# Attention over 96 token chunks: the maximum is subtracted inside the stream of the next logit and value products

## The chip, the core and the metric

The kernel runs on one core of a Trainium2 chip. The metric is the device time of one execution in microseconds (us), as the median of several runs. The engines of the core run side by side, each through its own list of instructions in order, and wait for one another by semaphores: TensorE (PE in the profile, its weight loads PEld), VectorE (DVE), ScalarE (ACT), GpSimd (POOL) and SyncE (SP).

## The reference, cut to what matters

The whole model is a chain of a convolution, a delta-rule attention, an expert-choice layer, an attention over video embeddings and a mixture of experts. The change lies in the attention over the video:

```
t = layer_norm(text_embeds, ln1_g, ln1_b)
vd = layer_norm(video_embeds, ln1_g, ln1_b)
q = (t @ Wq.T + bq).reshape(T, Nw, HEADS, HEAD_DIM)
k = (vd @ Wk.T + bk).reshape(V, Fr, HEADS, HEAD_DIM)
v = (vd @ Wv.T + bv).reshape(V, Fr, HEADS, HEAD_DIM)
logits = jnp.einsum('avhd,bthd->abhvt', k, q) / math.sqrt(HEAD_DIM)
weights = jax.nn.softmax(logits, axis=3)
attn = jnp.einsum('avhd,abhvt->abhtd', v, weights)
attn = attn.transpose(0, 1, 3, 2, 4).reshape(V, T, Nw, EMBED)
attn = attn.mean(axis=0)
o = attn @ Wo.T + bo
```

There are 64 videos (a) of 12 frames (v) and 2 heads (h) of 64. Each token takes a softmax over the 12 frames of every video and head, and the weighted values are averaged over the videos.

## The kernel before

`attention_phase` works on 96 chunks of 128 tokens (16 batches of 6 chunks). For one chunk the logits lie in three PSUM banks: the partitions are 2 heads times 64 videos, the free axis is 12 frames times 128 tokens. Two sets of three banks alternate from chunk to chunk; bank 6 gathers the products with the values, and bank 7 serves three purposes in turn: the transpose of normed tokens ("turn", line 367), the query projection (line 1667) and the output projection (lines 1726 and 1727).

The work on one chunk is spread over several steps, and each engine has a loop over the step n, written out by hand; there is no scheduler.

- TensorE, step n: for each of the 12 frames, the logits of chunk n (line 1689) and the products of chunk n-4 with the values (line 1697), as 64x64 pieces of the array side by side. Then, in the steps that have one, a turn or a query projection for a later batch. Then the subtraction of the maximum of chunk n-1 (line 1715): three products with an identity in bf16 add the negated maximum to the logits in PSUM ("shift" from here on). Then the output projection of chunk n-5, which writes bank 7.
- VectorE, step n: two small sums for the denominator of chunk n-2 (lines 1584, 1588), the negated maximum over the frames of chunk n (line 1592, it reads PSUM), and the product of the exponentials of chunk n-2 with the reciprocal denominator (line 1596, two inputs from SBUF).
- ScalarE, step n: the copy of chunk n-6's output (line 1628), the copy of chunk n-4's value sums out of bank 6 ("aT", line 1632), in some steps the copy of a turn (line 381, "a_xT") or of a query (line 1613, "qT") out of bank 7, then the three exponentials of chunk n-1 (line 1641), one for each bank, each released by one shift, then the reciprocal of chunk n-2's denominator (lines 1648, 1650), and in some steps the norm of tokens (line 1607).
- GpSimd: one addition for each chunk, of one half of its exponentials to the other (line 1661).

Turns stand in the steps n with n mod 12 = 1, 3, 7 or 9 and queries in those with n mod 12 = 2, 4, 8 or 10, as long as there is a next batch: 30 of each. Of any six steps in a row in the steady state two hold a turn, two a query and two neither ("plain" steps). Turn, query and output projection share bank 7, so in a step with a turn or a query the output projection waits until ScalarE has copied the bank out:

```
if now:
    pe.wait_ge(nt.moved, now[0] * 4 + now[1] + 1)
elif before:
    pe.wait_ge(q_ready, before[0] * 4 + before[1] + 1)
elif o:
    pe.wait_ge(o_ready, o)
```

Here `now` is a turn in this step, `before` a query, `nt.moved` counts the copies of line 381, `q_ready` those of line 1613. The output projection begins with n = 5.

Of the kernel before, what the change touches and what calls it, by code (L numbers as in the profile page):

```python
# [8 lines left out]
ACT = mybir.ActivationFunctionType  # L9
# [4 lines left out]
P = 128  # L14
# [8 lines left out]
NCH = B * NC  # L23
# [1501 lines left out]
def attention_phase(nc, k):  # L1525
# [6 lines left out]
    with stack:  # L1532
        nt = NormTranspose(nc, k, "a_", sb, sem)
        qT = sb("qT", [P, 2, TP])
        nm = sb("nm", [P, 2, P], BF16)
        eb = sb("eb", [P, 4, FR, P])
# [7 lines left out]
        q_ps, q_ready, q_bias, l_ps, m_ready, shifted, e_ready = (  # L1544
            sem(x) for x in ("q_ps", "q_ready", "q_bias", "l_ps", "nm_ready", "shifted", "e_ready"))
# [4 lines left out]
        FB = FR // 3  # L1550
# [5 lines left out]
        def lbanks(n):  # L1556
            o = 3 * (n % 2) * 512
            return k.psf[:, o:o + FR * P].rearrange("p (v t) -> p v t", t=P)
# [4 lines left out]
        def place(n, hd):  # L1563

            return half(hd if n // 4 % 2 == 0 else 1 - hd)
# [9 lines left out]
        with nc.Block() as block:  # L1575
# [25 lines left out]
            @block.scalar  # L1601
            def _(act):
                def norm(i, g):
                    for j in range(GC):
                        c = (g % 2) * GC + j
                        at = i * ST + (g // 2) * NC + c
                        last = nc.scalar.activation(nt.xl[:, g, j, :], k.h[:, i * 2 + g // 2, c, :], ACT.Identity,
                                                    scale=k.rstd[:, at:at + 1], bias=k.mean[:, at:at + 1])
                    last.then_inc(nt.normed, 1)

                def query(i, g, bank):
                    act.wait_ge(q_ps, i * 4 + g + 1)
                    nc.scalar.activation(qT[:, g // 2, (g % 2) * GW:(g % 2 + 1) * GW], k.ps[:, bank, 0:GW],
                                         ACT.Identity, scale=0.125, bias=bq8[:, 0:1]).then_inc(q_ready, 1)

                nc.scalar.preload_act_table_set("natural_log_exp_and_others")
                for g in range(2):
                    norm(0, g)
                for g in range(2):
                    nt.move(act, 0, g, 6 + g, k.g1[:, 0:1], k.b1n[:, 0:1])  # L1620
                act.wait_ge(q_bias, 2)
                for g in range(2):
                    query(0, g, 4 + g)
                for n in range(NCH + 6):
                    o = n - 6
                    if o >= 0:
                        act.wait_ge(o_ps, o + 1)
                        nc.scalar.activation(big[:, o, :], k.ps[:, 7, 0:P], ACT.Copy).then_inc(o_ready, 1)
                    a = n - 4
                    if 0 <= a < NCH:  # L1630
                        act.wait_ge(a_ps, a + 1)
                        nc.scalar.activation(aT[:, a % 2, :], k.ps[:, 6, 0:P], ACT.Copy).then_inc(a_ready, 1)
                    if slot(n):
                        nt.move(act, *slot(n), 7, k.g1[:, 0:1], k.b1n[:, 0:1])
                    if slot(n - 1):
                        query(*slot(n - 1), 7)
                    e = n - 1
                    if 0 <= e < NCH:
                        for s in range(3):
                            act.wait_ge(shifted, 3 * e + s + 1)  # L1640
                            nc.scalar.activation(eb[:, e % 4, s * FB:(s + 1) * FB], lbanks(e)[:, s * FB:(s + 1) * FB],  # L1641
                                                 ACT.Exp).then_inc(e_ready, 1)
                    w = n - 2
                    if 0 <= w < NCH:
                        act.wait_ge(summed, w + 1)
                        if w >= 2:
                            act.wait_ge(w_ready, w - 1)
                        nc.scalar.activation(rd[:, w % 2, :], den[:, w % 2, :], ACT.Ln).then_inc(logged, 1)
                        act.wait_ge(logged, w + 1)
                        nc.scalar.activation(rd[:, w % 2, :], rd[:, w % 2, :], ACT.Exp, scale=-1.0).then_inc(rd_ready, 1)  # L1650
                    if slot(n + 1):
                        norm(*slot(n + 1))
# [10 lines left out]
            @block.tensor  # L1663
            def _(pe):
                def query(i, g, bank):
                    pe.wait_ge(nt.moved, i * 4 + g + 1)
                    nc.tensor.matmul(k.ps[:, bank, 0:GW], k.wq[:, :], nt.xT[:, g // 2, (g % 2) * GW:(g % 2 + 1) * GW],
                                     start=True, stop=True).then_inc(q_ps, 1)

                for g in range(2):  # L1670
                    nt.turn(pe, 0, g, 6 + g)
                for g in range(2):
                    query(0, g, 4 + g)
                pe.wait_ge(q_bias, 2)
                for n in range(NCH + 5):
                    a = n - 4
                    logits, values = n < NCH, 0 <= a < NCH
                    if logits and n % NC == 0:
                        pe.wait_ge(q_ready, n // NC * 2 + 2)
                    if values:  # L1680
                        pe.wait_ge(w_ready, a + 1)
                        if a:
                            pe.wait_ge(a_ready, a)
                    for v in range(FR):
                        if logits:
                            if v % FB == 0 and n >= 2:
                                pe.wait_ge(e_ready, 3 * (n - 2) + v // FB + 1)
                            for hd in range(2):
                                last = nc.tensor.matmul(  # L1689
                                    lbanks(n)[place(n, hd), v, :], k.Kt[half(hd), v, :],  # L1690
                                    qT[half(hd), n // NC % 2, (n % NC) * P:(n % NC + 1) * P],
                                    start=(v % FB == 0), stop=True, skip_group_check=True)
                            if v == FR - 1:
                                last.then_inc(l_ps, 1)
                        if values:
                            for hd in range(2):
                                last = nc.tensor.matmul(  # L1697
                                    k.ps[half(hd), 6, 0:P], k.Vd[place(a, hd), v, half(hd)],
                                    eb[place(a, hd), a % 4, v, :], start=(v == 0), stop=(v == FR - 1))
                            if v == FR - 1:  # L1700
                                last.then_inc(a_ps, 1)
                    now, before, o = slot(n), slot(n - 1), n - 5
                    if now or before:
                        if o >= 1:
                            pe.wait_ge(o_ready, o)
                        if before:
                            query(*before, 7)
                        if now:
                            if o < 1 and n > 1:
                                pe.wait_ge(q_ready, now[0] * 4 + now[1])  # L1710
                            nt.turn(pe, *now, 7)
                    if 1 <= n <= NCH:
                        pe.wait_ge(m_ready, n)
                        for s in range(3):
                            nc.tensor.matmul(lbanks(n - 1)[:, s * FB:(s + 1) * FB, :], k.identb[:, :],
                                             nm[:, (n - 1) % 2, None, :].to_broadcast([P, FB, P]), start=False, stop=True,
                                             skip_group_check=True).then_inc(shifted, 1)
                    if 0 <= o < NCH:
                        pe.wait_ge(a_ready, o + 1)
                        if now:  # L1720
                            pe.wait_ge(nt.moved, now[0] * 4 + now[1] + 1)
                        elif before:
                            pe.wait_ge(q_ready, before[0] * 4 + before[1] + 1)
                        elif o:
                            pe.wait_ge(o_ready, o)
                        nc.tensor.matmul(k.ps[:, 7, 0:P], one[0:1, :], k.bo1[0:1, :], start=True, stop=False)
                        nc.tensor.matmul(k.ps[:, 7, 0:P], aT[:, o % 2, :], k.wo1[:, :],
                                         start=False, stop=True).then_inc(o_ps, 1)
# [655 lines left out]
```

## Time and profile before

| | |
|---|---|
| median of 3 runs | 2298.33 us (2295.48 to 2301.55) |
| the profiled execution | 2295.3 us |
| its span, first to last instruction | 2293.4 us |
| TensorE busy in the span | 2042.9 us (89%) |
| VectorE busy | 1628.5 us (71%) |
| ScalarE busy | 1075.9 us (47%) |
| GpSimd busy | 608.5 us (27%) |
| attention loop | from 1062 to 1543 us of the span |

These shares are averages over stages with different limits; the attention is some 480 us of the 2293. In the views of the timeline each row has the start, the length, the engine, the source line, the operation with its output and input, and the number of instructions merged; in brackets stands idle time of the engine ahead of it and what ended it. A group of x2 matmuls of line 1689 runs beside an equal group of line 1697, and 24 such pairs of groups make the logits and values of one step.

### The profile page before, as it was taken

Reading aid. Unit: us, or ns where it says so; the run is one execution under the profiler, and the core shown is the slowest. Engines: PE = TensorE matmul, PEld = TensorE weight load, DVE = VectorE, ACT = ScalarE, POOL = GpSimd, SP = SyncE. Lnnn points to the kernel's source line nnn. Section 1 sums busy time; section 2 is a strip of 40 time slices with the busy share of each in tenths; the row PEclk is TensorE's granted clock in tenths of the full one; section 3 lists DMA queues with packets and bytes.
Section 4 is the critical chain, followed back from the end, with each engine's and each line's share of the span. In section 5 each row is a group of like instructions: output and inputs, shape, how many; then the busy total and the mean of one; then the engine's idle time right before and its main releaser. Section 6 shows DMA issues by size and latency. Waiting matters only on the chain. (4 is left out here: it accounts for less than half of the span.)

```text
span 2293.4 us, 54841 instructions
## 1 busy us (share of the span) xinstructions
PE 2042.9 (89%) x20986; PEld 1801.0 (79%) x20986; DVE 1628.5 (71%) x4183; ACT 1075.9 (47%) x2698; POOL 608.5 (27%) x650
## 2 busy tenths in 40 slices
PE   6699999989747888986999999985999999999998
PEld 5488777778536878874777777775999999999998
DVE  4755556554583855665999999987777777777773
ACT  4433333332344555644666666642444444444443
POOL 0002222220025555511333333333212221221220
PEclk9799999999868999998999999997999999999999
DMA  8100000100211111100000000000000000000000
GB/s 184 42 1 12 11 11 11 15 8 1 76 56 40 42 34 40 41 10 2 3 3 3 3 3 3 3 2 1 8 8 14 7 7 14 7 7 14 7 8 14
DMA packets 80356, 44.52 MB, mean 19 GB/s; under 512 B 45800, under 2 KB 74024, under 8 KB 79752
## 3 DMA queue, kind: packets, MB, share of 16 engines
q1 hardware_dynamic: 74248, 29.53, 5.7%
q0 software_dynamic: 5888, 12.07, 2.0%
q8 instruction: 137, 2.24, 0.4%
q14 instruction: 83, 0.68, 0.1%
HBM read 27.20 MB, written 14.38 MB: 18 GB/s over the span
## 5 line engine op out<-in xcount | busy, mean ns | idle before, releaser
L2105 ACT ACTIVATE w<-banks,b 128x384 f32<-128x384 f32 (+1 forms) x512 | 259.7, 573 | 393.0 <-PE banks L2179 393.0
L2161 PE MATMUL banks<-w,w 128*128 128x128 f32 (+1 forms) x3072 | 364.1, 275 | 0.0
L2161 PEld LDWEIGHTS banks<-w,w 128*128 128x128 f32 (+1 forms) x3072 | 350.4, 189 | 9.1 <-issue 8.7
L1689 PE MATMUL banks<-qT,w 64*64 64x128 f32 x4608 | 272.2, 271 | 3.2 <-ACT eb L1641 2.4
L1697 PE MATMUL banks<-eb,w 64*64 64x128 f32 x4608 | 272.4, 271 | 0.2 <-DVE eb L1596 0.2
L1689 PEld LDWEIGHTS banks<-qT,w 64*64 64x64 f32 x4608 | 249.3, 133 | 16.6 <-DVE eb L1596 2.2
L1661 POOL TENSOR_TENSOR t<-eb 128x768 f32<-128x768 f32 x96 | 174.6, 1819 | 309.2 <-ACT eb L1641 299.3
L1697 PEld LDWEIGHTS banks<-eb,w 64*64 64x64 f32 x4608 | 249.2, 133 | 0.9 <-DVE eb L1596 0.8
L2002 DVE SCALAR_TENSOR_TENSOR h<-banks,t_wt,h 128x128 f32 (+3 forms) x672 | 183.8, 344 | 83.1 <-PE banks L2161 79.7
L1237 POOL DMA_INDIRECT xg<-xs,rowu x184 | 179.5, 976 | 127.0 <-DMA xg<-xs,rowu 84.7
L1596 DVE TENSOR_TENSOR eb<-eb,rd 128x1536 f32<-128x1536 f32 x96 | 208.6, 2172 | 2.1 <-ACT rd L1650 2.1
L2177 PE MATMUL banks<-t_xh,t_w1h 128*128 128x384 f32 (+1 forms) x512 | 182.5, 356 | 0.1
L1592 DVE TENSOR_REDUCE nm<-banks 128x128 bf16<-128x1536 f32 x96 | 167.8, 1748 | 10.8 <-PE banks L1689 10.8
L2179 PE MATMUL banks<-t_xh,t_w1l 128*128 128x384 f32 (+1 forms) x512 | 171.7, 335 | 0.0
L2178 PE MATMUL banks<-t_xlo,t_w1h 128*128 128x384 f32 (+1 forms) x512 | 171.0, 334 | 0.0
L2045 POOL TENSOR_TENSOR t_rstd<-t_nv,t_minus_half 128x6 f32<-128x6 f32 x48 | 63.6, 1326 | 399.7 <-DVE t_nv L1903 398.3
L1641 ACT ACTIVATE eb<-banks 128x512 f32<-128x512 f32 x288 | 150.5, 598 | 0.0
L1183 DVE SCALAR_TENSOR_TENSOR x_yl<-banks,gates,x_yh 128x128 fp32r<-128x128 f32 x184 | 52.0, 345 | 129.3 <-ACT x_yh L1330 129.1
L1428 PE MATMUL banks<-x_sel,x_yh 128*128 128x374 f32 (+1 forms) x384 | 119.7, 393 | 2.1 <-ACT x_oT L1339 1.9
L1191 DVE TENSOR_SCALAR x_sel<-iota,place 128x748 fp32r<-128x748 f32 x184 | 104.6, 622 | 6.3 <-PE banks L1428 6.2
L729 ACT ACTIVATE DT<-banks 128x768 f32<-128x768 f32 x60 | 48.7, 811 | 123.6 <-PE banks L822 123.6
L1428 PE MATMUL banks<-x_sel,x_yl 128*128 128x374 f32 (+1 forms) x384 | 98.8, 339 | 0.0
(300 smaller groups left out, 4325.3 us busy)
## 6 DMA issues: line engine op xcount, KB each, us to landing
out<-h SPq DMA_DIRECT2D x16, 320.0 KB
xs<-r_xl SPq DMA_DIRECT2D x16, 192.0 KB, 2.8
h<-in_xT SPq DMA_DIRECT2D x4, 750.0 KB, 14.8
h<-in_xT SPq DMA_DIRECT2D x4, 749.0 KB, 17.6
xg<-xs,rowu POOLq DMA_INDIRECT x184
xs<-r_xl SPq DMA_DIRECT2D x16, 128.0 KB
blocks<-NT SPq DMA_DIRECT2D x24, 48.0 KB, 1.9
D<-blocks SPq DMA_DIRECT2D x24, 48.0 KB, 2.1
```

Of the source, the lines that this page charges most:

```text
L1237: nc.gpsimd.indirect_dma_start(out=xg[:, 4 * g + j, :], out_offset=None, in_=k.xs, in_offset=bass.IndirectOffsetOnAxis(ap=rowu[:, col:col ...
L1428: last = nc.tensor.matmul(k.ps[:, 5 + s, 0:TW // 2], y[lo:hi, col % 8, :], sel[lo:hi, col % SEL, s * (TW // 2):(s + 1) * (TW // 2)], start ...
L1596: nc.vector.tensor_tensor(eb[:, w % 4], eb[:, w % 4], rd[:, w % 2, None, :].to_broadcast([P, FR, P]), ALU.mult).then_inc(w_ready, 1)
L1661: nc.gpsimd.tensor_tensor(t1[:, n % 2], e[:, 0:6], e[:, 6:12], ALU.add).then_inc(tree, 1)
L1689: last = nc.tensor.matmul(lbanks(n)[place(n, hd), v, :], k.Kt[half(hd), v, :], qT[half(hd), n // NC % 2, (n % NC) * P:(n % NC + 1) * P], s ...
L1697: last = nc.tensor.matmul(k.ps[half(hd), 6, 0:P], k.Vd[place(a, hd), v, half(hd)], eb[place(a, hd), a % 4, v, :], start=(v == 0), stop=(v ...
L2002: last = nc.vector.scalar_tensor_tensor(out=hh, in0=k.psf[0:n, o:o + P], scalar=wt[0:n, par, c * E1 + e:c * E1 + e + 1], in1=hh if e else ...
L2105: nc.scalar.activation(gb[u % 2][:, f, s * GW:s * GW + NFREE[s]], k.ps[:, order.bank(n), 0:NFREE[s]], ACT.Relu, bias=k.b1_1[:, 2 * e + f:2 ...
L2161: last = nc.tensor.matmul(k.psf[0:n, o:o + P], gb[u % 2][:, f, c * P:c * P + n], k.w2_1[:, 2 * e + f, :], start=(f == 0), stop=(f == 1))
L2177: nc.tensor.matmul(ps, w1h[:, 2 * e + f, :], xh[:, g, 0:w], start=True, stop=False)
L2178: nc.tensor.matmul(ps, w1h[:, 2 * e + f, :], xlo[:, g, 0:w], start=False, stop=False)
L2179: nc.tensor.matmul(ps, w1l[:, 2 * e + f, :], xh[:, g, 0:w], start=False, stop=True).then_inc(full, 1)
```

## The change

On TensorE the shift of chunk n-1 moves from behind the turn or query of step n into the loop over the frames: ahead of frame 8 of 12, the last third of the logits and values. It still waits for the same maximum. On ScalarE the three exponentials of chunk n-1 move ahead of the copies aT, a_xT and qT of the same step; only the output copy of line 1628 still stands ahead of them. For the first output projection (chunk 0), which followed a query of the step before, a wait for that query's copy is written out. Nothing is added to or taken from the arithmetic.

```diff
@@ scalar @@
                     a = n - 4
+                    e = n - 1
+                    if 0 <= e < NCH:
+                        for s in range(3):
+                            act.wait_ge(shifted, 3 * e + s + 1)
+                            nc.scalar.activation(eb[:, e % 4, s * FB:(s + 1) * FB], lbanks(e)[:, s * FB:(s + 1) * FB],
+                                                 ACT.Exp).then_inc(e_ready, 1)
                     if 0 <= a < NCH:
                         act.wait_ge(a_ps, a + 1)
                         nc.scalar.activation(aT[:, a % 2, :], k.ps[:, 6, 0:P], ACT.Copy).then_inc(a_ready, 1)
...
                     if slot(n - 1):
                         query(*slot(n - 1), 7)
-                    e = n - 1
-                    if 0 <= e < NCH:
-                        for s in range(3):
-                            act.wait_ge(shifted, 3 * e + s + 1)
-                            nc.scalar.activation(eb[:, e % 4, s * FB:(s + 1) * FB], lbanks(e)[:, s * FB:(s + 1) * FB],
-                                                 ACT.Exp).then_inc(e_ready, 1)
@@ tensor @@
+                def shift(e):
+                    pe.wait_ge(m_ready, e + 1)
+                    for s in range(3):
+                        nc.tensor.matmul(lbanks(e)[:, s * FB:(s + 1) * FB, :], k.identb[:, :],
+                                         nm[:, e % 2, None, :].to_broadcast([P, FB, P]), start=False, stop=True,
+                                         skip_group_check=True).then_inc(shifted, 1)
...
                     for v in range(FR):
+                        if v == 2 * FB and 1 <= n <= NCH:
+                            shift(n - 1)
                         if logits:
...
-                    if 1 <= n <= NCH:
-                        pe.wait_ge(m_ready, n)
-                        for s in range(3):
-                            nc.tensor.matmul(lbanks(n - 1)[:, s * FB:(s + 1) * FB, :], k.identb[:, :],
-                                             nm[:, (n - 1) % 2, None, :].to_broadcast([P, FB, P]), start=False, stop=True,
-                                             skip_group_check=True).then_inc(shifted, 1)
                     if 0 <= o < NCH:
...
                         elif o:
                             pe.wait_ge(o_ready, o)
+                        else:
+                            pe.wait_ge(q_ready, 4)
```

TensorE in step 7, the first steady step with a turn, in the kernel before. The names are the output and input tiles (`a_xl` the normed tokens, `nm` the negated maxima, `eb` the exponentials), `nm_ready` tells of a maximum, `a_moved` of a copy of a turn, `ao_ready` of an output copy:

```order
L1697 MATMUL banks<-eb,w_0 64x128 x2
L367 MATMUL banks<-ident,a_xl 128x128 [waits a_normed,ao_ready]
L367 MATMUL banks<-ident,a_xl 128x128 x2
L1715 MATMUL banks<-nm,identb 128x512 [waits nm_ready]
L1715 MATMUL banks<-nm,identb 128x512 x2
L1726 MATMUL banks<-bo,one 128x128 [waits a_moved,a_ready]
L1727 MATMUL banks<-wo,aT 128x128
```

The same step of TensorE in the changed kernel, from the shift on; the rows left out are the rest of the last third of logits and values:

```order
L1673 MATMUL banks<-nm,identb 128x512 [waits nm_ready]
L1673 MATMUL banks<-nm,identb 128x512 x2
L1698 MATMUL banks<-qT,w_0 64x128 [waits e_ready]
L1698 MATMUL banks<-qT,w_0 64x128
L1706 MATMUL banks<-eb,w_0 64x128 x2
...
L367 MATMUL banks<-ident,a_xl 128x128 [waits a_normed,ao_ready]
L367 MATMUL banks<-ident,a_xl 128x128 x2
L1731 MATMUL banks<-bo,one 128x128 [waits a_moved,a_ready]
L1732 MATMUL banks<-wo,aT 128x128
```

The shift no longer stands between the turn and the output projection that waits for the turn's copy; it now splits the run of 64-row products.

ScalarE in the same step before, where `shifted` tells of a shift, `a_ps` of finished value sums and `a_turned` of a turn:

```order
L1628 ACTIVATE o_all<-banks 128x128 [waits ao_ps]
L1632 ACTIVATE aT<-banks 128x128 [waits a_ps]
L381 ACTIVATE a_xT<-banks,b1n,g 128x384 [waits a_turned]
L1641 ACTIVATE eb<-banks 128x512 [waits shifted] x3
L1648 ACTIVATE rd<-den 128x128 [waits aw_ready,summed]
```

And in the changed kernel:

```order
L1628 ACTIVATE o_all<-banks 128x128 [waits ao_ps]
L1634 ACTIVATE eb<-banks 128x512 [waits shifted] x3
L1638 ACTIVATE aT<-banks 128x128 [waits a_ps]
L381 ACTIVATE a_xT<-banks,b1n,g 128x384 [waits a_turned]
L1648 ACTIVATE rd<-den 128x128 [waits aw_ready,summed]
```

The exponentials went past two copies, each of which TensorE waits for: aT in the next step, a_xT in this one.

## Rows read from the trace of the kernel before

**Rows 1.** Windows: length; busy us (count) of PE, PEld, DVE, ACT, POOL; granted clock; DMA.

```profile
850.00:900.00 50.00, 42.68 (x258) 38.84 (x258) 28.06 (x75) 26.72 (x80) 28.46 (x31) 0.97 0.15 40
...
1100.00:1500.00 400.00, 390.89 (x8558) 299.06 (x8554) 397.19 (x328) 268.44 (x707) 148.38 (x83) 1.00 0.01 3
```

**Rows 2.** Waits, 1100 to 1520: total us, times, longest.

```profile
PE banks L1726 <- ACT a_xT L381: 5.6, 27, 0.2
...
PEld banks L1715 <- DVE nm L1592: 0.5, 3, 0.2
```

**Rows 3.** Timeline of TensorE around a plain step.

```profile
1150.20 0.28 PE L1689 MATMUL banks<-qT,w 64*64 64x128 f32 x2
...
1150.42 0.82 PE L1715 MATMUL banks<-nm,identb 128*128 128x512 bf16 x3
1151.17 0.48 PE L1726 MATMUL banks<-bo,one 1*128 1x128 f32 x2
...
1152.01 0.33 PE L1689 MATMUL banks<-qT,w 64*64 64x128 f32 x2
...
1152.17 0.28 PE L1689 MATMUL banks<-qT,w 64*64 64x128 f32 x2
```

**Rows 4.** Timeline of TensorE and ScalarE in the next step, which has a turn.

```profile
1154.57 0.28 PE L1689 MATMUL banks<-qT,w 64*64 64x128 f32 x2
...
1154.88 0.55 PE L367 MATMUL banks<-ident,a_xl 128*128 128x128 f32 x3
...
1155.26 0.81 PE L1715 MATMUL banks<-nm,identb 128*128 128x512 bf16 x3
1155.46 0.67 ACT L381 ACTIVATE a_xT<-banks,b1n,g 128x384 f32<-128x384 f32 x1 [0.23 <-PE banks L367]
1156.04 1.56 ACT L1641 ACTIVATE eb<-banks 128x512 f32<-128x512 f32 x3
...
1156.28 0.45 PE L1726 MATMUL banks<-bo,one 1*128 1x128 f32 x2 [0.21 <-ACT a_xT L381]
```

**Rows 5.** Timeline of TensorE, then ScalarE, in the step after, which has a query.

```profile
1159.64 0.28 PE L1689 MATMUL banks<-qT,w 64*64 64x128 f32 x2
...
1159.86 0.91 PE L1667 MATMUL banks<-a_xT,wq 128*128 128x384 f32 x2
1160.61 0.81 PE L1715 MATMUL banks<-nm,identb 128*128 128x512 bf16 x3
1161.54 0.46 PE L1726 MATMUL banks<-bo,one 1*128 1x128 f32 x2
```
```profile
1160.81 0.58 ACT L1613 ACTIVATE qT<-banks,bq 128x384 f32<-128x384 f32 x1 [0.51 <-PE banks L1667]
```

**Rows 6.** Timeline of TensorE: the shifts of the last plain step and six steps after [rows 3].

```profile
1175.37 0.82 PE L1715 MATMUL banks<-nm,identb 128*128 128x512 bf16 x3
...
1179.73 0.82 PE L1715 MATMUL banks<-nm,identb 128*128 128x512 bf16 x3
```

**Rows 7.** One line's instructions: count, duration min/median/max in ns, first and last start.

```profile
L1596 DVE TENSOR_TENSOR eb<-eb,rd x96: 1742/2279/2930, 1076.2 to 1535.7; 128x1536 f32<-128x1536 f32 x96
```

**Rows 8.** Timeline of VectorE: maxima a step apart, then a stretched product; then GpSimd beside it.

```profile
1148.31 1.75 DVE L1592 TENSOR_REDUCE nm<-banks 128x128 bf16<-128x1536 f32 x1
...
1152.74 1.75 DVE L1592 TENSOR_REDUCE nm<-banks 128x128 bf16<-128x1536 f32 x1
...
1163.79 2.59 DVE L1596 TENSOR_TENSOR eb<-eb,rd 128x1536 f32<-128x1536 f32 x1
```
```profile
1162.93 1.82 POOL L1661 TENSOR_TENSOR t<-eb 128x768 f32<-128x768 f32 x1 [3.44 <-ACT eb L1641]
```

**Rows 9.** Costliest groups of the page: busy, mean ns, idle before and its enders.

```profile
L1689 PE MATMUL banks<-qT,w 64*64 64x128 f32 x4608 | 272.2, 271 | 3.2 <-ACT eb L1641 2.4
```

**Rows 10.** Timeline near the end of the loop: TensorE, then VectorE's last maximum.

```profile
1524.02 0.82 PE L1715 MATMUL banks<-nm,identb 128*128 128x512 bf16 x3
```
```profile
1526.62 1.75 DVE L1592 TENSOR_REDUCE nm<-banks 128x128 bf16<-128x1536 f32 x1
```

## The prediction

> **What bounds the kernel now.** I read the windows of the attention loop first, then the waits, then the timeline step by step. Over 400 us of the loop both TensorE (390.9 us) and VectorE (397.2 us) are busy almost without a gap, at full granted clock (1.00, the upper of the two levels, 2.4 GHz) [rows 1]. So the shares of busy time don't tell which of the two sets the pace. The waits do, together with the lengths. TensorE waits for VectorE's maximum 0.5 us in 420, and 5.6 us for ScalarE's copy of a turn [rows 2]; VectorE waits for nothing at all. Two engines can both run without a wait only if one of them is elastic, and the durations show which. TensorE's instructions keep their lengths from step to step. VectorE's product of line 1596 takes anything from 1.74 to 2.93 us [rows 7]: the one at 1163.79 took 2.59, and beside its first 0.96 us ran GpSimd's addition, which began at 1162.93 and took 1.82 [rows 8]. Without such an overlap VectorE needs 4.43 us a step (1148.31 to 1152.74) [rows 8]. GpSimd's start hangs on TensorE's shift by way of the exponentials. So when TensorE is late against VectorE, the addition slides under the product and slows VectorE down until the two have the same rate. TensorE's list of work sets the rate; VectorE adapts.
>
> TensorE's period is six steps, 29.31 us (shift at 1150.42 to shift at 1179.73) [rows 3, 6]: two steps with a turn, two with a query, two plain. A plain step takes 4.36 us (1175.37 to 1179.73) [rows 6], less than VectorE's undisturbed 4.43, so there the two are nearly even; the average of 4.885 comes from turns and queries.
>
> **What the change costs TensorE.** First the pieces. A pair of groups of logits and values takes 0.109 us (22 of them from 1152.17 to 1154.57) [rows 3, 4], so 24 pairs are 2.62 us and the last third 0.87. Going from them to the shift takes 0.22 instead of 0.11 (1150.20 to 1150.42), so the entry costs 0.11. The three shifts and the way on to the output projection take 0.75 (1150.42 to 1151.17). The first pair after 128-row work takes 0.16 (1152.01 to 1152.17), so the way back costs 0.05 [rows 3]. No row shows a shift followed by a pair; I take 0.75 plus 0.05.
>
> In a *plain* step the shift moves, nothing is hidden by it, and one change of form is added: the values now go straight to the output projection, at 0.11 more as in the steps with a query (1159.64 to 1159.86) [rows 5], and the shift has a way back of 0.05. That is +0.16.
>
> In a step with a *turn* the shift is cover today. The turn begins at 1154.88, the shift at 1155.26, the copy a_xT at 1155.46, and the output projection, which needs the copy, at 1156.28: 1.40 us after the turn began [rows 4]. Without the shift TensorE would be ready 0.38 after the turn began, and the copy can't begin sooner, since it began 0.03 after the turn ended. So the 1.40 stay, about 1.0 of them idle, and the shift's time is added in full where it now stands: 0.11 + 0.75 + 0.05 = +0.91. In a step with a *query* it is the same: query at 1159.86, copy qT at 1160.81, output projection at 1161.54, 1.68 us in all [rows 5], in which the shift of 0.75 was hidden and now isn't: +0.91.
>
> Steps: 30 turns and 30 queries, of which the first two of each lie ahead of the first output projection (step 5) and wait for no copy. That leaves 56 steps at 0.91 = 51.0 us, and of the 91 steps from 5 to 95 there are 35 plain ones at 0.16 = 5.6 us. Six steps would take 29.31 + 4 x 0.91 + 2 x 0.16 = 33.3 us.
>
> **What it gains, and what is hidden.** The exponentials come sooner, by a third of a step or more. TensorE waits for them only at the start of the loop, 2.4 us in all [rows 9]; that goes, less 4 x 0.16: -1.8. At the end VectorE's last maximum begins 2.6 us after the shift that follows the last logits (1526.62 against 1524.02) [rows 10], because VectorE is behind. With TensorE slower VectorE has caught up by then and begins about 0.3 after the logits: -2.3, less up to 0.84 (2.59 against 1.75) [rows 8] if the last addition meets a product: -1.5.
>
> On ScalarE the exponentials now stand ahead of aT, a_xT and qT. Let the shift begin at X. The first of the three ends at X + 0.38 (0.81 for all, at a spacing of 0.22), and the exponentials take 1.56 [rows 4], to about X + 2.0. TensorE ends the last third at X + 0.75 + 0.05 + 0.87 = X + 1.67, begins the turn at about X + 1.9, and a_xT is due 0.58 after that, X + 2.45. In between there is room for aT, so neither copy is late. I cost this part at nothing; the cover is some 0.2 us, and if it failed each late 0.1 us would cost 5.6 us over the 56 steps. The shift's wait for the maximum also comes sooner: after a plain step it stands 0.84 + 0.05 + 1.75 + 0.11 = 2.75 us behind the logits, and the maximum takes 1.75 [rows 8]. 1.0 us is left as long as VectorE isn't behind, and at 4.43 us of work against an average step of 5.5 it isn't. The wait that is written out for the first output projection is for a copy made a step before: nothing. No DMA is issued in the loop.
>
> Sum: 51.0 + 5.6 - 1.8 - 1.5 = +53.3. The profiled execution took 2295.3 us and would take 2348.6; the median of the three runs lies 3.0 above it, at 2298.3, and becomes 2351.6.
>
> The entry of the shift takes 0.11 and the way back from 128-row work 0.05 [rows 3]. The Trainium skill, "TensorEngine Tiling (Array Packing)", section "Key Properties", says that a change of the tiling mode drains TensorE, and it makes no difference between the two directions. The trace agrees that a change costs something and shows the way back as the cheaper one. If the return from the shift cost as much as the entry, 0.06 more in 91 steps would make the sum +59.
>
> *Bounds.* From below: the three shifts at their bare spacing, 0.65, and no cost of changing form, 36 us in the 56 steps and nothing in the plain ones, less 4 at the ends: 2330. From above: a return at 0.15 and aT late by 0.1 make 1.11 in the 56 steps and 0.26 in 35, +71 and -2 at the ends, 2367; and if the idle in each step brought the granted clock to the 0.97 of the stretch where TensorE is busy 85% [rows 1], 3% of some 26 us of streaming in 15 periods adds 11: about 2375.
>
> **Rivals.** *VectorE is the bound (faster).* It is busy 99% of the loop, TensorE's weight loads 299 of 400 us [rows 1]. Then what counts is that GpSimd's addition starts sooner and meets the maximum, which reads PSUM, instead of the product: every step falls to 4.43, 0.455 less in the 84 steps from 5 to 88, -38, or 2260 us. It decides if TensorE has half a microsecond a step to spare. Against it: the maximum that was ready at 1154.49 was used only at 1155.26 [rows 8, 4], and TensorE waited for a maximum 0.5 us in 420 [rows 2]. The Trainium skill, "Perfetto Trace Analysis", section "Identifying the Most-Contended Engine", would have it this way: it judges VectorE by its occupancy and TensorE by its weight loads, not by its matmuls' busy time. I give it 0.08.
>
> *The copies come sooner (no change).* If ScalarE, rid of the exponentials ahead of the output projection, copied bank 7 earlier by the shift's 0.75, nothing would be lost, and the time stays at about 2299. Against it: a_xT follows the turn at once today and qT the query [rows 4, 5]. 0.05.
>
> *The clock falls (slower still).* With about 1 us of idle in four steps of six TensorE's clock might be granted at its lower level for a part. A tenth of the streaming is 2.6 us a period, 38 in all: about 2390. The stretch at 85% has 0.97, though [rows 1]. 0.05.
>
> **How the numbers follow.** The forecast has 0.82, and its bounds, 2330 to 2375, are the range, which leaves the rivals outside. A measurement of this kernel can tell about 0.3% (7 us) from no change. Slower 0.87 (forecast and clock), the same 0.05, faster 0.08.
>
> **What would show it.** In the profile of the changed kernel: six steps in 33.3 us, plain ones 4.5; the waits of the output projection for a_xT and for qT at about 1 us each, 28 times each; the turn still 1.40 ahead of it and the query 1.68; the product of line 1596 mostly near 1.75; idle time of VectorE ahead of the maximum, ended by the logits. The forecast is wrong if the six steps take less than 29.3 us, if the output projection follows the turn sooner than 1.4 us, or if TensorE stands waiting for the maximum ahead of the shift.

## The result, and the profile after

The changed kernel takes 2351.8 us (median of 4 runs, 2346.5 to 2357.3) against 2297.5 us for the kernel before: a ratio of 1.0231, 95% interval 1.0213 to 1.0249. That is 54 us slower; 2352 was forecast.

The profiled execution has a span of 2352.6 us against 2293.4. Of the 59.2 us more, 5.5 lie ahead of the attention loop, where the program is the same: the loop's first turn begins at 1063.4 in place of 1057.9. From that turn to the end of the last output copy the loop takes 538.6 us in place of 485.0, which is +53.6, and what follows the loop takes 750.5 in both. So the change costs 53.6 us, all of it in the loop.

The window that answers to the last of [rows 1], with the same columns:

```profile
1100.00:1500.00 400.00, 361.20 (x7573) 260.45 (x7571) 331.38 (x292) 242.23 (x628) 130.22 (x72) 1.00 0.01 3
```

VectorE was busy 397 us of these 400 before and is now 331; TensorE fell from 391 to 361. The clock is still granted in full. Now VectorE is the one that waits, and the waits between 1100 and 1570 say for whom (total us, times, longest; line 1698 holds the logits, 1731 the output projection):

```profile
DVE nm L1592 <- PE banks L1698: 70.4, 56, 1.3
...
PE banks L1731 <- ACT a_xT L381: 23.9, 28, 0.9
...
PE banks L1731 <- ACT qT L1613: 21.4, 28, 0.8
```

Where TensorE waited 5.6 us for the copies of turns [rows 2], it waits 23.9, and 21.4 for the copies of queries, 28 times each. The timeline of TensorE through a step with a turn and on to the next with a query, to be read beside [rows 4, 5]; line 1673 is the shift:

```profile
1194.61 0.82 PE L1673 MATMUL banks<-nm,identb 128*128 128x512 bf16 x3
...
1198.91 0.28 PE L1698 MATMUL banks<-qT,w 64*64 64x128 f32 x2
...
1199.13 0.82 PE L1673 MATMUL banks<-nm,identb 128*128 128x512 bf16 x3
1199.88 0.33 PE L1698 MATMUL banks<-qT,w 64*64 64x128 f32 x2
...
1200.70 0.28 PE L1698 MATMUL banks<-qT,w 64*64 64x128 f32 x2
...
1200.92 0.55 PE L367 MATMUL banks<-ident,a_xl 128*128 128x128 f32 x3
...
1202.32 0.45 PE L1731 MATMUL banks<-bo,one 1*128 1x128 f32 x2 [0.85 <-ACT a_xT L381]
...
1205.03 0.82 PE L1673 MATMUL banks<-nm,identb 128*128 128x512 bf16 x3
...
1206.82 0.91 PE L1667 MATMUL banks<-a_xT,wq 128*128 128x384 f32 x2
1208.49 0.45 PE L1731 MATMUL banks<-bo,one 1*128 1x128 f32 x2 [0.76 <-ACT qT L1613]
```

The output projection still comes 1.40 us after the turn begins (1200.92 to 1202.32) and 1.67 after the query (1206.82 to 1208.49), as before. But the shift no longer fills that time, and takes 0.75 of its own (1199.13 to 1199.88). A plain step lasts 4.52 (1194.61 to 1199.13). The same step on ScalarE:

```profile
1199.56 1.57 ACT L1634 ACTIVATE eb<-banks 128x512 f32<-128x512 f32 x3 [0.87 <-PE banks L1673]
1201.08 0.28 ACT L1638 ACTIVATE aT<-banks 128x128 f32<-128x128 f32 x1
1201.51 0.67 ACT L381 ACTIVATE a_xT<-banks,b1n,g 128x384 f32<-128x384 f32 x1
```

The exponentials are over at 1201.13, aT follows at once, and a_xT begins at 1201.51, 0.59 after the turn: ScalarE's new order delays nothing. Six steps, from the shift at 1165.93 to that at 1199.13, take 33.20 us in place of 29.31:

```profile
1165.93 0.82 PE L1673 MATMUL banks<-nm,identb 128*128 128x512 bf16 x3
```

### The profile page after: what moved, and what is told of

Same layout as the page of the kernel before. It is cut to its first block and busy times, and to the rows that moved or that the text cites. A ratio compares the mean times of both kernels' runs of the same rounds, so it can differ in the third digit from the quotient of the medians.

```text
span 2352.6 us, 54842 instructions
## 1 busy us (share of the span) xinstructions
PE 2061.3 (88%) x20986; PEld 1794.6 (76%) x20986; DVE 1607.0 (68%) x4183; ACT 1079.9 (46%) x2698; POOL 607.0 (26%) x650
## 5 line engine op out<-in xcount | busy, mean ns | idle before, releaser
L1698 PE MATMUL banks<-qT,w 64*64 64x128 f32 x4608 | 292.8, 273 | 0.8 <-ACT qT L1613 0.8
L1706 PE MATMUL banks<-eb,w 64*64 64x128 f32 x4608 | 292.6, 273 | 0.0
L1596 DVE TENSOR_TENSOR eb<-eb,rd 128x1536 f32<-128x1536 f32 x96 | 176.8, 1841 | 8.4 <-ACT rd L1650 8.4
```

The source lines that it names most:

```text
L1596: nc.vector.tensor_tensor(eb[:, w % 4], eb[:, w % 4], rd[:, w % 2, None, :].to_broadcast([P, FR, P]), ALU.mult).then_inc(w_ready, 1)
L1698: last = nc.tensor.matmul(lbanks(n)[place(n, hd), v, :], k.Kt[half(hd), v, :], qT[half(hd), n // NC % 2, (n % NC) * P:(n % NC + 1) * P], s ...
L1706: last = nc.tensor.matmul(k.ps[half(hd), 6, 0:P], k.Vd[place(a, hd), v, half(hd)], eb[place(a, hd), a % 4, v, :], start=(v == 0), stop=(v ...
```

## Experiments

Two theories run through the first runs. By the forecast's, TensorE's list of work sets the pace and VectorE's product stretches until it fits. By the rival's, VectorE is the bound, as its busy share suggests. Periods of six steps are read from the starts of the shifts in each trace, between steps 24 and 84, and "the loop" is measured as above (485.0 in the trace of the kernel before).

**Half of VectorE's product.**

```diff
-                        nc.vector.tensor_tensor(eb[:, w % 4], eb[:, w % 4],
-                                                rd[:, w % 2, None, :].to_broadcast([P, FR, P]),
+                        nc.vector.tensor_tensor(eb[:, w % 4, 0:6], eb[:, w % 4, 0:6],
+                                                rd[:, w % 2, None, :].to_broadcast([P, 6, P]),
```

> The kernel before, with VectorE's product of line 1596 on 6 of the 12 frames only; the other 6 frames' exponentials stay without their reciprocal denominator, so part of the computation is left out. VectorE has about 0.8 us less to do in each of 96 steps. Theory (TensorE's list sets the pace, VectorE adapts): six steps stay at 29.3 us, the time within 3 us of the kernel before, and VectorE shows idle time instead of stretched products. Rival (VectorE is the bound): its step falls from 4.885 to about 4.1 or less until TensorE's plain 4.4 holds it, so 35 to 45 us less.

Measured: 2302.6 against 2303.8 us, ratio 0.999 (0.9976 to 1.0005). Six steps take 29.23, the loop 485.7. VectorE isn't the bound. One part of what was expected is wrong: the halved product mostly stays long. First its row over the whole loop (count, duration min/median/max in ns, first and last start), then one of them in the timeline and GpSimd's addition beside it:

```profile
L1596 DVE TENSOR_TENSOR eb<-eb,rd x96: 958/2133/2148, 1088.4 to 1545.6; 128x768 f32<-128x768 f32 x96
```
```profile
1199.02 2.14 DVE L1596 TENSOR_TENSOR eb<-eb,rd 128x768 f32<-128x768 f32 x1 [0.18 <-ACT rd L1650]
```
```profile
1198.53 1.82 POOL L1661 TENSOR_TENSOR t<-eb 128x768 f32<-128x768 f32 x1 [3.26 <-ACT eb L1641]
```

Alone it takes 0.96 us. With the addition over its first 1.33 us it takes 2.14. VectorE, with less to do, moves ahead of TensorE until more of the product lies under the addition, and so looks busy again. That is the elasticity of the forecast, caught in the act.

**A lighter bias for TensorE.**

```diff
-        one = sb("one", [1, P])
+        one = sb("one", [P, P], BF16)
+        bo2 = sb("bo2", [P, P], BF16)
+        boh = sb("boh", [P, P], BF16)
...
+                nc.vector.memset(bo2[:], 0.0).then_inc(q_bias, 1)
+                nc.vector.tensor_copy(boh[:], k.bo1[:, :]).then_inc(q_bias, 1)
+                dve.wait_ge(q_bias, 4)
+                nc.vector.tensor_copy(bo2[0:1, :], boh[0:1, :]).then_inc(q_bias, 1)
+                nc.vector.tensor_tensor(bo2[32:33, :], k.bo1[32:33, :], boh[32:33, :], ALU.subtract).then_inc(q_bias, 1)
...
-                        nc.tensor.matmul(k.ps[:, 7, 0:P], one[0:1, :], k.bo1[0:1, :], start=True, stop=False)
+                        nc.tensor.matmul(k.ps[:, 7, 0:P], one[:, :], bo2[:, :], start=True, stop=False)
```

> The kernel before, with the bias of the output projection added by one bf16 product of 128 rows (high and low part of the bias in two rows) in place of the two-pass fp32 product: TensorE has about 0.3 us less to do in each of 96 steps, VectorE nothing less. Theory (TensorE sets the pace): six steps fall from 29.3 by up to 1.8, to 27.5; VectorE undisturbed needs 26.6, and with some overlap left I expect 28.0 to 28.7, so 9 to 20 us less in all. Rival (VectorE is the bound): no change, within 3 us.

Measured: 2286.0 against 2303.8, ratio 0.9916 (0.9894 to 0.9937), 18 us less. Six steps take 28.36, the loop 473.7. Work taken from TensorE pays, work taken from VectorE doesn't. It pays about half of what is taken (0.95 of some 1.8 us in six steps), because VectorE, still partly under the addition (its product has a median of 1.99), can't follow all the way: between 1100 and 1520 the matmuls of the logits now wait for the product 33 times, 15.6 us in all.

**The two halves of the change apart.** TensorE's half alone leaves out the first two hunks of the diff:

> One half of the change: TensorE's shift ahead of the last third, ScalarE's order as in the kernel before. Theory (the loss is the shift's lost cover on TensorE): turn and query steps lengthen as in the changed kernel, the output projection still follows a turn by 1.40 and a query by 1.67, so at least +53; and as the exponentials wait behind the copies, GpSimd's addition falls onto VectorE's product again, which can cost more: six steps 33.2 to 34.5, +53 to +80. Rival (it is ScalarE's new order that costs): near the kernel before, within 10 us.

Measured: 2378.0 against 2303.8, ratio 1.0324 (1.0303 to 1.0344), the loop 561.6, so 23 us more than the whole change. Six steps take 34.16. TensorE's part of the timeline, from one plain step's shift through the next step with a turn (line 1688 is the shift, 1728 the output projection), and the product's durations:

```profile
1207.14 0.82 PE L1688 MATMUL banks<-nm,identb 128*128 128x512 bf16 x3 [0.25 <-DVE nm L1592]
1208.92 0.55 PE L367 MATMUL banks<-ident,a_xl 128*128 128x128 f32 x3
1210.32 0.45 PE L1728 MATMUL banks<-bo,one 1*128 1x128 f32 x2 [0.85 <-ACT a_xT L381]
```
```profile
L1596 DVE TENSOR_TENSOR eb<-eb,rd x96: 1757/2933/2942, 1082.8 to 1616.8; 128x1536 f32<-128x1536 f32 x96
```

The turn is 1.40 ahead of the output projection again, and turn and query steps are as long as in the whole change. What is added sits in the plain steps (4.93 and 5.09 in place of 4.53): the exponentials, behind the copies, are late, the addition falls onto the product (median 2.93), and now TensorE waits for the maximum ahead of the shift (first row above). So ScalarE's half of the change is a repair: it brings the product back to 1.84 and saves these 23 us.

ScalarE's half alone leaves out TensorE's hunks but for the last wait:

> The other half: ScalarE's exponentials ahead of its copies, TensorE's shift where it was, behind the turn or query. Theory: the copies aT, a_xT and qT now wait for exponentials that start only after the shift; the output projection comes about 2 us later in steps with a turn or a query, and the next values about 0.6 later in plain ones, so six steps take 37 to 39 us and the loop some 110 to 135 us more. So the two halves need one another, and the second earns nothing by itself. Rival (starting the exponentials sooner is worth something of itself): no slower than the first half alone.

Measured, in one run: 2487.4, the loop 669.7, +185 and more than expected. Where the clock was granted in full the six steps from 1363.12 to 1401.41 take 38.3, inside what was expected. But the clock wasn't granted in full throughout. An output projection behind a query, with the idle time ahead of it, and two windows with the columns of [rows 1]:

```profile
1387.01 0.45 PE L1728 MATMUL banks<-bo,one 1*128 1x128 f32 x2 [1.96 <-ACT qT L1613]
```
```profile
1363.12:1401.41 38.29, 28.71 (x630) 22.00 (x628) 30.87 (x25) 19.15 (x52) 10.85 (x6) 1.00 0.01 3
...
1438.40:1612.00 173.60, 136.59 (x2444) 107.85 (x2440) 118.92 (x94) 74.41 (x203) 42.44 (x24) 0.84 0.01 2
```

TensorE idles 2 us at a time and is busy 75% of the first window, at 1.00. That window lies in a stretch of 82 us at the upper level. Before it, from 1110 to 1345, and again in the second window the clock goes back and forth between the two levels (2.4 and 1.2 GHz), so that the mean granted is 0.84 over the second window; six steps there take 44.4 to 46.2. From 1601 to the end of the loop it is at 1.00 again, and six steps take 38.1. This is the forecast's third rival, met in another kernel; what makes the clock change between these stretches of one program stays open.

**The cover alone, without splitting the stream.**

```diff
+                    if 1 <= n <= NCH:
+                        pe.wait_ge(m_ready, n)
+                        for s in range(3):
+                            nc.tensor.matmul(lbanks(n - 1)[:, s * FB:(s + 1) * FB, :], ...
                     if now or before:
...
                             nt.turn(pe, *now, 7)
-                    if 1 <= n <= NCH:
-                        pe.wait_ge(m_ready, n)
-                        for s in range(3):
-                            nc.tensor.matmul(lbanks(n - 1)[:, s * FB:(s + 1) * FB, :], ...
```

> The kernel before, with the shift behind the last frame but ahead of the turn or query; ScalarE's order is left. No stream is split, only the cover goes. Theory: plain steps stay at 4.4, turn and query steps lengthen by the shift's 0.75 less what was idle anyway: six steps at 32.0 to 32.4, 38 to 46 us more than the kernel before. Rival (the split costs): within 10 us of the kernel before.

Measured: 2331.5 against 2297.3, ratio 1.0152 (1.0135 to 1.0169), 34 us; the loop 518.5, +33.5. Six steps take 31.54, a little under the expected 32.0 to 32.4. Plain steps are 4.37. TensorE in a step with a turn (line 1706 is the shift):

```profile
1206.23 0.82 PE L1706 MATMUL banks<-nm,identb 128*128 128x512 bf16 x3
1206.89 0.49 PE L367 MATMUL banks<-ident,a_xl 128*128 128x128 f32 x3
...
1208.24 0.45 PE L1726 MATMUL banks<-bo,one 1*128 1x128 f32 x2 [0.85 <-ACT a_xT L381]
```

A shift followed by a turn takes 0.66, and the turn is then 1.35 ahead of the output projection, so that the lost cover is 0.56 a step ((31.54 - 29.31) / 4) and not 0.75. In the changed kernel a turn or query step lost 0.89. No run splits the stream and keeps the cover, so the remaining 0.33 is put down to the split by difference. The rows account for 0.30 of it: the shift takes 0.75 in place of 0.66, the way back to the pairs 0.05 and the second entry 0.11, and the turn is 1.40 ahead of the output projection in place of 1.35.

**The split alone.**

```diff
-                        if v == 2 * FB and 1 <= n <= NCH:
-                            shift(n - 1)
+                        if v in (8, 9, 10) and 1 <= n <= NCH:
+                            shift(n - 1, v - 8)
```

> The changed kernel, with its three shifts apart: one each ahead of frames 8, 9 and 10, where all three stood ahead of frame 8. The work is the same; the stream of 64-row products is left and entered three times a step instead of once. It prices a change of form alone. By the pieces of the prediction one more change there and back costs 0.11 going in and 0.15 coming out, 0.26 in all, so two more make a plain step 5.05 in place of 4.53 and six steps 36.3 in place of 33.2. If a change of form costs nothing of itself, plain steps stay at 4.53; if the way back costs a full 0.2 like the entry, they reach 5.2 or more.

Measured, in one run: 2401.8; the loop 592.4, 53.8 more than with the shifts together. Plain steps take 5.06, six steps 36.40. TensorE through the first of the three:

```profile
1208.00 0.28 PE L1698 MATMUL banks<-qT,w 64*64 64x128 f32 x2
...
1208.22 0.39 PE L1673 MATMUL banks<-nm,identb 128*128 128x512 bf16 x1
...
1208.54 0.33 PE L1698 MATMUL banks<-qT,w 64*64 64x128 f32 x2
...
1208.70 0.28 PE L1698 MATMUL banks<-qT,w 64*64 64x128 f32 x2
...
1208.92 0.39 PE L1673 MATMUL banks<-nm,identb 128*128 128x512 bf16 x1
```

From the last pair ahead of the shift to the shift 0.22, to the next pair 0.32, to the one after 0.16: 0.70 in place of 0.11 + 0.22 + 0.11, where 0.11 is a pair and 0.22 a shift's spacing. One change of form there and back costs 0.26 us. Twice that in 96 steps is 50 us, most of the 53.8.

**The wait taken out of the changed kernel.** The output projection goes ahead of the turn or query, and ScalarE copies it out first:

```diff
-                    o = n - 6
-                    if o >= 0:
-                        act.wait_ge(o_ps, o + 1)
-                        nc.scalar.activation(big[:, o, :], k.ps[:, 7, 0:P], ACT.Copy).then_inc(o_ready, 1)
...
+                    o = n - 5
+                    if 0 <= o < NCH:
+                        act.wait_ge(o_ps, o + 1)
+                        nc.scalar.activation(big[:, o, :], k.ps[:, 7, 0:P], ACT.Copy).then_inc(o_ready, 1)
                     if slot(n):
...
                     if now or before:
-                        if o >= 1:
-                            pe.wait_ge(o_ready, o)
+                        if o >= 0:
+                            pe.wait_ge(o_ready, o + 1)
```

> The changed kernel, with one thing more: the output projection goes ahead of the turn or query of its step, and ScalarE copies it out before it copies the turn or query, so TensorE no longer waits for a copy out of bank 7 that was filled just before. The split of the logits and values by the shift stays. Theory (most of the loss is the wait that the shift used to cover, 45 us in the trace of the changed kernel; the changes of form are about 0.16 a step): plain steps stay at 4.5, six steps fall from 33.2 to 29.5 to 30.2, and the time lies 3 to 15 us above the kernel before. Rival (it is the split of the 64-row products, or VectorE and ScalarE, that cost): it stays more than 35 us above.

Measured: 2327.7 against 2297.3, ratio 1.0138 (1.0121 to 1.0155): 30 us above the kernel before, 24 us better than the change. Six steps take 31.55, not 29.5 to 30.2, and the time lies between the theory's 3 to 15 us and the rival's 35. The step shows why (line 1718 is the output projection):

```profile
1202.32 0.48 PE L1718 MATMUL banks<-bo,one 1*128 1x128 f32 x2
...
1203.59 0.55 PE L367 MATMUL banks<-ident,a_xl 128*128 128x128 f32 x3 [0.37 <-ACT o_all L1638]
```

The wait isn't gone. The turn and the query now wait for the output's copy, 0.37 us of idle time, since they write the same bank 7. With the shift no longer there to stand between, both orders of the two users of bank 7 that were run leave TensorE waiting.

**A better order.** If that is so, the shift belongs between the two users: output projection, shift, turn or query. It would then cover the output's copy, and the next step's logits the turn's copy. The rest of the order is the kernel before, with ScalarE's copies as aT, output, exponentials, turn or query:

```diff
                     if 0 <= o < NCH:
                         pe.wait_ge(a_ready, o + 1)
-                        if now:
-                            pe.wait_ge(nt.moved, now[0] * 4 + now[1] + 1)
-                        elif before:
-                            pe.wait_ge(q_ready, before[0] * 4 + before[1] + 1)
+                        if before:
+                            pe.wait_ge(nt.moved, before[0] * 4 + before[1] + 1)
+                        elif slot(n - 2):
+                            turned = slot(n - 2)
+                            pe.wait_ge(q_ready, turned[0] * 4 + turned[1] + 1)
...
+                    if 1 <= n <= NCH:
+                        pe.wait_ge(m_ready, n)
...
                     if now or before:
```

> The kernel before, with the output projection first behind the values, then the shift, then the turn or query; ScalarE copies the output out ahead of its exponentials and the turn or query behind them. No engine's work changes. Theory: the 0.2 to 0.3 us that TensorE still waits in turn and query steps go, and the shift covers the output's copy: six steps at 28.6 to 29.0 in place of 29.3, 5 to 10 us less. Rival (the exponentials, now later against the logits by the output projection's 0.84, throw GpSimd's addition onto VectorE's product so far that VectorE becomes the bound): slower than before.

Measured: 2289.9 against 2297.3, ratio 0.9965 (0.9951 to 0.9979); the loop 474.1, six steps 28.53. That is 7 us less, as expected, and the six steps are a little under the expected 28.6 to 29.0. In its trace, between 1100 and 1520, the output projection waits for no copy any more, and turns and queries wait for the output's copy 0.2 us at most. What TensorE still waits for is VectorE's product (31.0 us in 51 waits of the logits' weight loads) and the exponentials (11.1 us in 32). With the lighter bias on top:

> The order of the run before, with the bias as one bf16 product as well: TensorE is relieved twice. Theory: six steps at 27.0 to 27.6, near VectorE's undisturbed 26.6, 25 to 36 us less than the kernel before. Rival (VectorE's overlap with GpSimd keeps it at the pace that the light bias alone gave): 28.3, about 18 us less.

Measured: 2256.9 against 2297.3, ratio 0.9834 (0.9811 to 0.9858), 40 us less than the kernel before and 95 less than the change. Six steps take 26.57, the loop 446.4. This is better than expected, and VectorE is now the bound: the product (line 1603 here) is almost always undisturbed, and TensorE waits for it.

```profile
L1603 DVE TENSOR_TENSOR eb<-eb,rd x96: 1740/1748/2462, 1075.9 to 1496.2; 128x1536 f32<-128x1536 f32 x96
...
who waited for it (us, times):
  PEld banks L1696: 44.5, 77
  PE banks L1696: 18.2, 50
```

26.57 is six times VectorE's undisturbed 4.43 [rows 8].

## Why the prediction was right, point by point

*TensorE sets the pace.* Shown: half of VectorE's product away changes the time by a factor of 0.999, 0.3 us a step away from TensorE by 0.9916.

*VectorE adapts.* Shown by the halved product that stays at 2.13 us, and by the median of the product in the changed kernel, 1.84 in place of 2.28 [rows 7], with idle time ahead of the maximum. The forecast's "mostly near 1.75" was a little low.

*Turn and query steps +0.91, plain +0.16.* Plain steps measure 4.53, as 4.37 + 0.16. Four turn and query steps add 33.20 - 29.31 - 2 x 0.16 = 3.57 in six steps, 0.89 each. The 1.40 and 1.67 stayed, with 0.85 and 0.76 of idle time in them rather than about 1.0. The entry took 0.22, the shift 0.75, and the first pair after it 0.16. That 0.75 holds from a shift to a pair was luck: the forecast had only the row from a shift to an output projection and said so. The +59 that a dearer return would have given is not borne out. Counted from the bare shifts (0.65) the way out is 0.15 and the way in 0.11, so a change of form costs in both directions. This agrees with the Trainium skill's "TensorEngine Tiling (Array Packing)", section "Key Properties", by which a change of the tiling mode drains TensorE.

The 0.02 a step that are missing have a cause that the forecast left out: in the kernel before, one turn of every two waited about 0.1 us more than the other for the output copy of the step before, and in the changed kernel none does. The waits of the turn's weight load, before (1100 to 1520), then after (1100 to 1570):

```profile
PEld banks L367 <- ACT o_all L1628: 3.4, 13, 0.3
...
PEld banks L367 <- issue: 2.4, 14, 0.2
```
```profile
PEld banks L367 <- issue: 4.8, 28, 0.2
```

*The split of the +0.91 into causes* is better known now than in the forecast. Without any split the lost cover is 0.56 a step (+33.5 in the loop); the other 20 of the 53.6 are, by difference, the split of the stream. The forecast's sum held because the pieces were taken in the order in which the changed kernel has them.

*ScalarE's new order delays no copy, with 0.15 us to spare.* a_xT began 0.59 after the turn and 0.15 after aT's end (1201.36 to 1201.51); the forecast had some 0.2. But the forecast saw only what this half might cost. It is worth 23 us: without it the change costs 74.

*The ends, and some luck in the sum.* The two traces of the kernel before and the changed one tell the loop's parts. From the loop's first turn to the first logits of step 5 (at 1084.3 and 1088.6) they take 26.43 and 25.12 us, so -1.3 where -1.8 was forecast. From there to the first logits of step 95 (1521.2 and 1580.5) they take 436.89 and 491.96, +55.1 where 51.0 + 5.6 = 56.6 was forecast. The rest takes 21.67 and 21.54, -0.1 where -1.5 was forecast: VectorE's lateness had cost TensorE little there, since steps 95 to 98 took 4.42, 4.43, 3.90 and 3.60 us before and 4.53, 4.50, 3.60 and 3.60 after. So the steps came out 1.5 lower and the ends 1.9 higher than forecast, and that the loop's 53.6 lies so near 53.3 is in part luck.

*The range.* Its upper end has a slip: 2367 and 11 make 2378, not 2375. Nothing hangs on it.

*The rivals.* VectorE as the bound fell with the halved product. There the Trainium skill's "Perfetto Trace Analysis", "Identifying the Most-Contended Engine", which takes VectorE's occupancy at its word, differs from the runs, and the runs decide: 99% of occupancy was partly stretched time. The copies did not come sooner. The clock stayed at 1.00 through the window of the changed kernel, busy 90%, and among all runs it fell between 1100 and the end of the loop only in the one with ScalarE's half alone.

## What to carry to other kernels

When two engines are both busy all the time, look which one's instructions change their length: that one may be adapting while the other sets the pace, and a run with less work on each of them tells. Before moving an instruction away from a place, ask which wait it fills there: between two users of one bank the shift cost next to nothing here, and ahead of both it cost 0.56 us of its 0.65 even without splitting a stream. If such a filler is to be used better, change what stands on either side of it.

## What the runs showed of the hardware

A product on VectorE with two inputs in SBUF nearly stands still while GpSimd adds two SBUF inputs: 0.96 us of work under 1.33 us of overlap took 2.14, and 1.74 us took 2.93 with about 1.3 of overlap, while the addition stays at 1.82. In the traces of the kernel before, the changed one and TensorE's half alone, overlaps of 0.33, 0.65, 0.97 and 1.32 us made the product 0.18, 0.52, 0.83 and 1.18 us longer, the overlap less about 0.14 each time, and one of 0.11, in the run with the wait taken out, made it no longer. In all these pairs the addition had begun first. A bf16 product for the bias, one instruction, in place of a fp32 one, which the trace shows as two, makes a step 0.3 us shorter (4.51 to 4.20 where VectorE doesn't hold it). TensorE's clock stayed at its upper level where it idled under 1 us at a time and was busy 90%; with 2 us at a time it held the upper level through some stretches, busy 75%, and went back and forth between the two levels in others. Against the 38.3 us of six steps at the upper level the mean of 42.75 from step 24 to 84 makes that some 45 us in ten periods, an estimate from one run.
